# Experts' weights copied from a held set by ScalarE in place of a DMA load per block, from the tenth block on

## The chip, the cores and the metric

The kernel runs on one core of a Trainium2 chip. The metric is device time of one execution in microseconds: 2009.96 us before, the median of three runs (2009.22 to 2015.2). TensorE (PE), VectorE (DVE), ScalarE (ACT), GpSimd (POOL) and SyncE (SP) run their own instruction streams and meet through semaphores. SP and POOL issue the DMA transfers spoken of here.

## The reference

A two-layer graph network over 6250 nodes and 200,000 edges, and behind it a mixture of six experts, with two chosen per node. Cut to what matters:

```python
x = x + gnn(layernorm(x), edges)               # two layers, segment sums over edges
f = layernorm(x)
logits = softmax(relu(f @ router_w1 + b1) @ router_w2 + b2)
top_w, top_i = top_k(logits, 2)
gate = softmax(top_w)
h1 = relu(f @ expert_w1[e] + expert_b1[e])     # 256 -> 256, per expert
h2 = relu(h1 @ expert_w2[e] + expert_b2[e])
out_e = h2 @ expert_w3[e] + expert_b3[e]
x = x + gate[0] * out_e(top_i[0]) + gate[1] * out_e(top_i[1])
```

Everything is float32 at the interface. The change touches the experts' part, the last three products.

## The kernel before

The graph layers come first. Their message sums are products of count matrices with the messages, which the tile `parts` holds in SBUF ([128, 49, 512] in float16). During the sums of the second layer the router works beside them, pair of node tiles by pair, and scatters every node's row twice, into `first_rows` for its first choice and `second_rows` for its second, sorted by expert.

The experts then work in blocks of 256 rows of one expert: 60 blocks, 30 for the first choices (blocks 0 to 29, results scattered to `first_out`) and 30 for the second (blocks 30 to 59, whose base rows are gathered from `first_out` and whose results go to the output). `block_table` in SBUF says for each block its expert and its first row. It is known only at run time, so a table read into a register precedes each use of it.

All of one block's weights and biases are 1796 float32 columns of a packed table in DRAM (`expert_pack`): 514 for the first layer, 514 for the second, 768 for the third with its bias. The tile `w`, a view of a part of the tile `counts_again` that is free by then, has three slots, so block b uses slot b % 3. `rows` has six slots.

On each engine the blocks run skewed. In step b:

- TensorE (`products`, L2166): first layer of block b+2 (from `y_t`, L2126), transposes of block b+3 (`turn`, L2120), second layer of block b+1 (from `h_t`, L2126), third layer of block b (`outs`, L2155).
- ScalarE (`low_halves`, L2211): the lower half of the first layer of block b+2 with bias and relu (`low`, L2202), the copy of `y_t` for block b+3 (`y_copy`, L2198), the lower half of the second layer of block b+1 (L2202).
- VectorE (`high_halves`, L2362): the upper halves (L2320), the token indices (L2342, L2344), bias and base rows (L2325), the normalised rows of block b+4 in the first half (L2349), the gated result (`add_outs`, L2333), which sets `result_ready`.
- GpSimd (`moves`, L2419): two indirect scatters a block, and in the second half two gathers (L2409, L2416).
- SyncE (`loads`, L2080): four transfers in this order, each behind a table read: first weights of block b+5 (`first_weights`, once the first layer of b+2 has been read out of PSUM), second weights of block b+4 (`second_weights`, likewise), third weights of block b+3 and the rows of block b+6 (`load_rows`), both behind `result_ready` of block b.

Semaphore counts order the engines; no planner reorders anything, the order on each engine is the one written. During the first twelve steps `beside(b)` puts the last of the routing between the blocks' instructions: on ScalarE the router's last root, copy, relu and two exponentials in steps 2, 3, 4, 6 and 7. The loops run six blocks a trip; the first twelve blocks and the ends are written out.

Of the kernel before, what the change touches and what calls it, by code (L numbers as in the profile page):

```python
# [17 lines left out]
P = 128  # L18
# [448 lines left out]
def gnn_moe_kernel(nc, x, src, dst, gnn_w, gnn_b, res_w, res_b, router_w1, router_b1, router_w2, router_b2,  # L467
# [35 lines left out]
    with ctx:  # L503
# [765 lines left out]
        def gather_sum(l):  # L1269
# [5 lines left out]
            rows_t_ready = own_sem(f"rows_t_ready{l}")  # L1275
            hs_gathered = own_sem(f"hs_gathered{l}")
            agg_gathered = own_sem(f"agg_gathered{l}")
            summed = own_sem(f"summed{l}")
# [15 lines left out]
            with nc.Block() as block:  # L1294
# [23 lines left out]
                @block.tensor  # L1318
                def _(pe):
                    with pe.Fori(0, cols) as c:  # L1320
                        pe.wait_ge(column_made, ADDED * c + INDEXED)
                        nc.tensor.transpose(bank[0][:, 0:P], gs_dst[:, 0:1].to_broadcast([P, P]), ident[:, :]).then_inc(rows_t_ready, 1)
                        pe.wait_ge(column_made, ADDED * c + SAME)
                        pe.wait_ge(hs_gathered, 16 * c + 16)
                        nc.tensor.matmul(bank[1][:, 0:dim], gs_same[:, :], gs_hs[:, :], start=True, stop=True).then_inc(summed, 1)
# [8 lines left out]
                @block.vector  # L1334
                def _(dve):
                    dve.wait_ge(edges_back, 64)
                    dve.wait_ge(lower_set, 4)
                    with dve.Fori(0, cols) as c:
                        dve.wait_ge(scattered, 16 * c + 16)
                        nc.vector.tensor_copy(index[:, 0:1], src_sb[:, bass.ds(c, 1)]).then_inc(column_made, 1)  # L1340
                        nc.vector.tensor_copy(index[:, 1:2], dst_sb[:, bass.ds(c, 1)]).then_inc(column_made, 1)
                        nc.vector.tensor_copy(gs_dst[:, :], dst_sb[:, bass.ds(c, 1)]).then_inc(column_made, 1)
                        dve.wait_ge(rows_t_ready, c + 1)
                        nc.vector.tensor_scalar(gs_same[:, :], bank[0][:, 0:P], gs_dst[:, 0:1], None, ALU.is_equal).then_inc(column_made, 1)
                        dve.wait_ge(column_made, ADDED * c + SAME)

                        nc.vector.tensor_tensor(gs_before[:, :], gs_same[:, :], lower[:, :], ALU.mult).then_inc(column_made, 1)
                        dve.wait_ge(column_made, ADDED * c + SAME + 1)
                        nc.vector.tensor_reduce(gs_count[:, :], gs_before[:, :], AX, ALU.add).then_inc(column_made, 1)
                        dve.wait_ge(column_made, ADDED * c + SAME + 2)  # L1350
                        nc.vector.scalar_tensor_tensor(gs_count[:, :], gs_count[:, :], float(FAR), gs_dst[:, :], ALU.mult, ALU.add).then_inc(column_made, 1)
                        dve.wait_ge(column_made, ADDED * c + SAME + 3)
                        nc.vector.tensor_copy(index[:, 2:3], gs_count[:, :]).then_inc(column_made, 1)
                        dve.wait_ge(summed, c + 1)
                        dve.wait_ge(agg_gathered, 16 * c + 16)
                        nc.vector.tensor_tensor(gs_agg[:, :], gs_agg[:, :], bank[1][:, 0:dim], ALU.add).then_inc(column_made, 1)
# [602 lines left out]
        def expert_blocks(router, counts):  # L1959
# [13 lines left out]
            acc, result = (both_w[:, l, :, :] for l in range(2))  # L1973
            rows = sb("rows", [P, SB, 2, 2 * dim + 6], F32)
# [24 lines left out]
            rows_loaded = [sem(f"rows_loaded{b}") for b in range(SB)]  # L1999
            normal_ready = sem("normal_ready")  # L2000
# [16 lines left out]
            assert NB % SB == 0 and SB % WB == 0 and SB % 6 == 0  # L2017
# [24 lines left out]
            class Work:  # L2042
# [36 lines left out]

                def loads(self, sp):  # L2080
                    def after(first):
                        def body(b, k):
                            if not (isinstance(b, int) and b + 2 + WB >= BLOCKS):
                                self.first_weights(sp, b + 2, k + 2)
                            if not (isinstance(b, int) and b + 1 + WB >= BLOCKS):
                                self.second_weights(sp, b + 1, k + 1)
                            if isinstance(b, int) and b + WB >= BLOCKS:
                                return
                            e = self.expert_of(sp, b + WB)
                            sp.wait_ge(result_ready, b + 1)  # L2090
                            self.load_weights(sp, e, k, 2)
# [3 lines left out]
                            if first is not None:  # L2095
                                self.load_rows(sp, b + SB, k, first)
# [8 lines left out]
                    for b in range(BLOCKS - SB, BLOCKS):  # L2105
                        after(None)(b, b)
# [104 lines left out]
                def low_halves(self, act, beside):  # L2211
# [5 lines left out]

                    def steps(r, last=False):
                        for k in range(SB):
# [3 lines left out]
                            if not (last and k + 3 >= SB):  # L2223
                                self.y_copy(act, b + 3, (k + 3) % SB)
                            if not (last and k + 1 >= SB):
                                second(b + 1, (k + 1) % SB)
                            if isinstance(b, int) and b < 2 * SB:
                                beside(b)
# [373 lines left out]
```

## Time and profile before

| what | value |
|---|---|
| median of three runs | 2009.96 us (2009.22 to 2015.2) |
| the profiled execution | 2009.25 us |
| its span | 2006.8 us |
| TensorE busy | 1843.3 us, 92% of the span |
| VectorE busy | 1121.0 us, 56% |
| ScalarE busy | 769.0 us, 38% |
| GpSimd busy | 391.2 us, 19% |
| DMA | 412.57 MB, mean 206 GB/s |
| the experts' stage | from about 1610 us to the end, 60 blocks |

The busy shares are averages over stages with different limits. The sums of the graph layers fill the first 1600 us, mostly with TensorE; the change lies in the last 400. Times in the rows are microseconds from the span's start. In a row, `out<-in` names tiles with buffer numbers left out, so `h_t` is the first or the second layer's output and `counts_again` in the experts' stage is the weights' tile. "Issue" marks idle time for which the profile shows no releaser, and "remote" a releaser on another core or an unknown queue.

### The profile page before, as it was taken

To read this page: it belongs to the slowest core of one execution; us is meant where nothing else is said; L and a number is where in the kernel's file an instruction comes from. 1 tells how busy PE (TensorE), PEld (TensorE's weight loads), DVE (VectorE), ACT (ScalarE), POOL (GpSimd) and SP (SyncE) were. 2 spreads that over 40 slices of the span, in tenths; PEclk is the share of its full clock that TensorE was granted. 3 is DMA by queue.
4 is the path that set the end of the run, shared out by engine and by line. 5 is a ranking of instruction groups with operands and counts; after the bars stand their busy time and mean duration, and the time that the engine had idled before them with its cause. 6 is when DMAs were issued, how large, how long until landed. Compare 5 with 4: busy or idle time off the path is not lost. (4 is left out here: it accounts for less than half of the span.)

```text
span 2006.8 us, 35596 instructions
## 1 busy us (share of the span) xinstructions
PE 1843.3 (92%) x11170; PEld 1127.9 (56%) x11170; DVE 1121.0 (56%) x2788; ACT 769.0 (38%) x1686; POOL 391.2 (19%) x403
## 2 busy tenths in 40 slices
PE   4448799999999999999969999999999999989886
PEld 4337655555555555555524444454444478877775
DVE  7247766666666666666513444444444568644443
ACT  2226655665556565556501222222222232222221
POOL 1680000000000000000000112111112123346655
PEclk8679799999999999999979999999999999999998
DMA  6255498899889953323284445554444578877884
GB/s 223 58 85 114 130 322 301 296 349 262 288 283 291 305 179 127 152 88 154 109 324 160 176 170 188 192 203 178 170 175 176 190 230 250 257 220 230 249 246 125
DMA packets 139199, 412.57 MB, mean 206 GB/s; under 512 B 16552, under 2 KB 76928, under 8 KB 132856
## 3 DMA queue, kind: packets, MB, share of 16 engines
q1 hardware_dynamic: 100216, 283.65, 41.3%
q0 software_dynamic: 37904, 124.85, 21.2%
q10 hardware_dynamic: 1008, 3.21, 0.4%
q8 instruction: 33, 0.54, 0.1%
q14 instruction: 38, 0.31, 0.1%
HBM read 201.60 MB, written 219.99 MB: 210 GB/s over the span
## 5 line engine op out<-in xcount | busy, mean ns | idle before, releaser
L1380 PE MATMUL bank<-parts,counts 128*128 128x512 f16 x2401 | 644.4, 379 | 0.0
L1380 PE MATMUL bank<-parts,counts_again 128*128 128x512 f16 x2401 | 540.4, 381 | 17.4 <-DMA counts_again<-counts_table 17.4
L1544 ACT ACTIVATE counts<-bank 128x392 f16<-128x392 f32 x800 | 394.8, 497 | 312.9 <-PE bank L1460 306.2
L1380 PEld LDWEIGHTS bank<-parts,counts_again 128*128 128x128 f16 x2401 | 234.0, 99 | 286.9 <-issue 16.2
L595 DVE TENSOR_TENSOR rows_lo<-pair_keys,iota_lo 128x2048 bf16<-128x2048 bf16 x200 | 244.9, 1224 | 238.5 <-PE bank L1460 238.2
L1460 PEld LDWEIGHTS bank<-rows_hi,rows_lo 128*128 128x128 bf16 x3200 | 229.5, 99 | 202.5 <-issue 27.6
L1460 PE MATMUL bank<-rows_hi,rows_lo 128*128 128x98 bf16 x3200 | 280.0, 211 | 9.5 <-DVE rows_hi L595 8.6
L1380 PEld LDWEIGHTS bank<-parts,counts 128*128 128x128 f16 x2401 | 192.7, 96 | 103.9 <-issue 1.7
L454 POOL DMA_INDIRECT first_rows<-route_rows,route_spot_i x49 | 47.7, 973 | 839.9 <-DVE tokens L445 831.9
L595 DVE TENSOR_TENSOR rows_hi<-pair_keys,iota_hi 128x1568 bf16<-128x1568 bf16 x200 | 193.5, 967 | 0.0
L2202 ACT ACTIVATE h_t<-bank,counts_again 128x256 f32<-128x256 f32 x120 | 56.6, 473 | 210.2 <-PE bank L2126 147.2
L2126 PE MATMUL bank<-h_t,counts_again 128*128 128x256 f32 x480 | 119.1, 393 | 10.6 <-issue 6.6
L912 PE MATMUL bank<-both_w,feat 128*128 128x256 f32 x196 | 64.4, 461 | 60.5 <-issue 37.3
L1396 ACT ACTIVATE middle<-bank 128x256 f32<-128x256 f32 x98 | 37.2, 380 | 213.7 <-PE bank L1380 213.7
L2126 PE MATMUL bank<-y_t,counts_again 128*128 128x256 f32 x480 | 113.8, 380 | 4.7 <-issue 4.7
L2155 PE MATMUL bank<-counts_again,h_t 128*128 128x256 f32 x480 | 114.2, 381 | 0.0
L2320 DVE TENSOR_SCALAR h_t<-bank,counts_again 128x256 f32<-128x256 f32 x120 | 57.6, 480 | 93.7 <-PE bank L2126 48.3
L2126 PEld LDWEIGHTS bank<-h_t,counts_again 128*128 128x128 f32 x480 | 89.5, 196 | 22.5 <-issue 12.0
L2126 PEld LDWEIGHTS bank<-y_t,counts_again 128*128 128x128 f32 x480 | 90.8, 190 | 18.5 <-issue 6.3
L2155 PEld LDWEIGHTS bank<-counts_again,h_t 128*128 128x128 f32 x480 | 91.8, 192 | 12.8
L375 DVE TENSOR_TENSOR route_prob<-bank,router_b_sb 128x12 f32<-128x12 f32 (+1 forms) x25 | 4.2, 170 | 162.6 <-PE bank L365 162.6
L183 PE MATMUL bank<-both_w,x_t 128*128 128x512 f32 x196 | 92.3, 593 | 0.5 <-ACT x_t L173 0.5
(259 smaller groups left out, 1846.6 us busy)
## 6 DMA issues: line engine op xcount, KB each, us to landing
counts_table<-counts SPq DMA_DIRECT2D x25, 3136.0 KB, 10.7
counts_again<-counts_table SPq DMA_DIRECT2D x24, 3136.0 KB, 11.3
first_rows<-zero_rows POOLq DMA_DIRECT2D x3, 10530.0 KB, 58.2
second_rows<-zero_rows POOLq DMA_DIRECT2D x3, 10449.0 KB, 66.7
counts_again<-expert_pack SPq DMA_DIRECT2D x120, 257.0 KB
counts_again<-expert_pack SPq DMA_DIRECT2D x60, 384.0 KB
res_tile<-res_table SPq DMA_DIRECT2D x98, 128.0 KB, 6.2
first_rows<-zero_rows POOLq DMA_DIRECT2D x1, 10270.0 KB, 58.6
```

The source lines that it names most:

```text
L183: mm = nc.tensor.matmul(self.product_bank[:, :], self.x1_t[:, o, k * P:(k + 1) * P], self.both_w[:, self.l + 1, k, :], start=k == 0, stop= ...
L454: pool.indirect_dma_start(table, bass.IndirectOffsetOnAxis(ap=self.spot_i[:, b, c, o:o + 1], axis=0), rows[:, b, o, lo:hi], None, bounds_c ...
L595: return nc.vector.tensor_tensor(rows, k, v, ALU.is_equal)
L912: mm = nc.tensor.matmul(res_bank(t)[:, 0:dim], feat[:, t, k * P:(k + 1) * P], both_w[:, 0, k, dim:2 * dim], start=k == 0, stop=k == K2 - 1)
L1380: mm = nc.tensor.matmul(acc[:, 0:2 * dim], lhs, rhs, start=s == 0, stop=s == tiles)
L1396: nc.scalar.activation(middle[:, o, :], bank[half_bank + o][:, dim:2 * dim], ACT.Copy, scale=1.0 / LOW).then_inc(middle_out, 1)
L1460: mm = nc.tensor.matmul(bank[4 + q % 4][:, u * width:(u + 1) * width], rows_lo[:, r % 2, at, :, u % 2], rows_hi[:, r % 2, at, :, u % 2], s ...
L1544: nc.scalar.activation(counts[:, b, :, :].rearrange("p s (o n) -> p o s n", o=2)[:, :, :, q * QUAD:(q + 1) * QUAD], bank[4 + q % 4][:, 0:Q ...
L2126: mm = nc.tensor.matmul(to[m][:, 0:ROWS], weights_of(k, n)[:, kf, m * P:(m + 1) * P], source[:, k % 2, kf, :], start=kf == 0, stop=kf == K ...
L2155: mm = nc.tensor.matmul(outs_bank[k % 2][:, cols_of], h2_t[:, k % 2, kf, h * P:(h + 1) * P], weights_of(k, 2)[:, kf, :], start=kf == 0, st ...
L2202: nc.scalar.activation(to[:, k % 2, 0, :], frm[0][:, 0:ROWS], ACT.Relu, bias=bias_of(k, n, 0)).then_inc(low_out, 1)
L2320: nc.vector.tensor_scalar(to[:, k % 2, 1, :], frm[1][:, 0:ROWS], bias_of(k, n, 1), 0.0, ALU.add, ALU.max).then_inc(high_out, 1)
```

## The change

A tile view `held` is laid over `parts`, which the sums no longer need: the packed weights of all six experts, 6 x 1796 float32 columns. SyncE loads one expert's weights behind each of the blocks 0 to 5. The weights of blocks 0 to 8 (`LOADED` = 9) are loaded by DMA as before. From block 9 on ScalarE copies a block's three parts from `held` into its slot of `w`, each copy behind a table read of its own, and signals the semaphores that the DMA signalled. SyncE is left with the rows loads. In the branch that is not taken here (a fallback for graphs with many equal edges) two semaphores become one, which frees the number for `held_loaded`.

```diff
+            held = parts[:, :, :].rearrange("p t d -> p (t d)").bitcast(F32)[:, 0:experts * W_COLS].rearrange("p (e n) -> p e n", e=experts)
+            LOADED = 3 * WB
...
+                def hold(self, sp, e):
+                    sp.dma_start(held[:, e, :], expert_pack[e]).then_inc(held_loaded, 16)
...
                         def body(b, k):
-                            if not (isinstance(b, int) and b + 2 + WB >= BLOCKS):
+                            if isinstance(b, int) and b + 2 + WB < LOADED:
                                 self.first_weights(sp, b + 2, k + 2)
-                            if not (isinstance(b, int) and b + 1 + WB >= BLOCKS):
+                            if isinstance(b, int) and b + 1 + WB < LOADED:
                                 self.second_weights(sp, b + 1, k + 1)
-                            if isinstance(b, int) and b + WB >= BLOCKS:
-                                return
-                            e = self.expert_of(sp, b + WB)
-                            sp.wait_ge(result_ready, b + 1)
-                            self.load_weights(sp, e, k, 2)
+                            if isinstance(b, int) and b + WB < LOADED:
+                                e = self.expert_of(sp, b + WB)
+                                sp.wait_ge(result_ready, b + 1)
+                                self.load_weights(sp, e, k, 2)
+                            else:
+                                sp.wait_ge(result_ready, b + 1)
...
-                            if first is not None:
-                                self.load_rows(sp, b + SB, k, first)
+                            self.load_rows(sp, b + SB, k, first)
+                            if isinstance(b, int) and b < experts:
+                                self.hold(sp, b)
...
+                    def weights(b, k, n):
+                        e = act.value_load(block_table[0:1, 0, bass.ds(b, 1)], min_val=0, max_val=experts - 1)
+                        if isinstance(b, int) and b == LOADED:
+                            act.wait_ge(held_loaded, 16 * experts)
+                        if n == 0:
+                            act.wait_ge(h1_high_out, b - (WB - 1))
+                        if n == 1:
+                            act.wait_ge(h2_high_out, b - (WB - 1))
+                        if n == 2:
+                            act.wait_ge(result_ready, b - (WB - 1))
+                        part = slice(W_AT[n], W_AT[n + 1])
+                        nc.scalar.activation(w[:, k % WB, part], held[:, bass.ds(e, 1), part].rearrange("p a n -> p (a n)"),
+                                             ACT.Copy).then_inc(w_loaded[n][k % WB], 16)
+
+                    def held_weights(b, k, n, last):
+                        if not (isinstance(b, int) and b < LOADED) and not (last and k >= SB):
+                            weights(b, k, n)
...
                             if not (last and k + 3 >= SB):
                                 self.y_copy(act, b + 3, (k + 3) % SB)
+                            held_weights(b + 4, k + 4, 0, last)
                             if not (last and k + 1 >= SB):
                                 second(b + 1, (k + 1) % SB)
+                            held_weights(b + 3, k + 3, 1, last)
+                            held_weights(b + 2, k + 2, 2, last)
```

Three places show how the order moves. An "ISA" row is register work or a wait of the instruction stream itself, a "TENSOR_LOAD" is a table read.

The first is ScalarE's loop of six blocks a trip, one step of it. Before:

```order
L2202 ACTIVATE h_t<-bank,counts_again 128x256 [waits h1_ready]
L2197 REGISTER_ALU
L2198 ACTIVATE y_t<-bank 128x512 [waits y_turned]
L2202 ACTIVATE h_t<-bank,counts_again 128x256 [waits h2_ready]
L2201 ISA
```

The same step in the changed kernel, without its last five rows, which are a third copy of 128x768 with its table read and a wait for `result_ready`:

```order
L2207 ACTIVATE h_t<-bank,counts_again 128x256 [waits h1_ready]
L2202 REGISTER_ALU
L2203 ACTIVATE y_t<-bank 128x512 [waits y_turned]
L2224 ISA
L2224 TENSOR_LOAD block_table
L2224 ISA x2
L2234 ISA [waits h1_high_out]
L2234 ACTIVATE counts_again<-parts 128x514
L2207 ACTIVATE h_t<-bank,counts_again 128x256 [waits h2_ready]
L2224 TENSOR_LOAD block_table
L2224 ISA x2
L2234 ISA [waits h2_high_out]
```

One copy now stands between the copy of `y_t` and the second layer's half, two behind that half.

The second is ScalarE in the step of block 5 of the changed kernel, which is written out and holds the first use of the held weights:

```order
L2207 ACTIVATE h_t<-bank,counts_again 128x256 [waits h1_ready]
L2203 ACTIVATE y_t<-bank 128x512 [waits y_turned]
L2224 TENSOR_LOAD block_table
L2224 ISA x2
L2234 ISA [waits h1_high_out,held_loaded]
L2234 ACTIVATE counts_again<-parts 128x514
L2207 ACTIVATE h_t<-bank,counts_again 128x256 [waits h2_ready]
```

The wait for `held_loaded`, all six loads, stands ahead of the second layer's half of block 6.

The third is SyncE in the same step of the changed kernel (`parts<-expert_pack` is the load of one expert's held weights; this is the sixth):

```order
L2049 TENSOR_LOAD block_table
L2049 ISA x2
L2053 ISA [waits result_ready]
L2053 DMA counts_again<-expert_pack 128x768
L2056 TENSOR_LOAD block_table
L2056 ISA x2
L2058 ISA
L2058 DMA rows<-first_rows 128x2x260
L2083 DMA parts<-expert_pack 128x1796
```

The sixth load is issued behind `result_ready` of block 5, block 8's third weights and a rows load. From the next step on SyncE's queue holds only a wait, a table read and the rows load for each block.

## Rows read from the trace of the kernel before

**Rows 1.** Busy time of each engine by stretch, granted clock, DMA share:

```profile
core 0: us, PE busy (x) PEld busy (x) DVE busy (x) ACT busy (x) POOL busy (x), PEclk, DMA share, GB/s
1620.00:1660.00 40.00, 38.34 (x194) 32.90 (x194) 28.67 (x106) 13.14 (x27) 15.92 (x16) 1.00 0.73 223
1690.00:1798.00 108.00, 108.00 (x539) 95.14 (x539) 66.07 (x188) 29.32 (x57) 40.84 (x40) 1.00 0.84 252
1800.00:1820.00 20.00, 14.74 (x64) 12.39 (x64) 7.80 (x21) 2.94 (x7) 14.12 (x14) 0.83 0.52 152
1812.00:1979.00 167.00, 147.74 (x700) 124.79 (x700) 72.05 (x200) 36.95 (x75) 103.13 (x101) 0.98 0.81 244
```

**Rows 2.** Timeline of TensorE (start, length, line, tiles, idle time before):

```profile
1618.52 1.89 PE L2126 MATMUL bank<-y_t,counts_again 128*128 128x256 f32 x8
...
1655.73 1.89 PE L2126 MATMUL bank<-y_t,counts_again 128*128 128x256 f32 x8
...
1657.89 1.89 PE L2126 MATMUL bank<-h_t,counts_again 128*128 128x256 f32 x8
...
1691.77 1.89 PE L2126 MATMUL bank<-y_t,counts_again 128*128 128x256 f32 x8
...
1798.54 1.89 PE L2126 MATMUL bank<-y_t,counts_again 128*128 128x256 f32 x8
...
1806.12 3.75 PE L2126 MATMUL bank<-h_t,counts_again 128*128 128x256 f32 x8 [5.26 <-issue]
...
1811.83 1.89 PE L2126 MATMUL bank<-y_t,counts_again 128*128 128x256 f32 x8
...
1979.07 1.89 PE L2126 MATMUL bank<-y_t,counts_again 128*128 128x256 f32 x8
```

**Rows 3.** Waits, 1800 to 1985 us (waiter, releaser: total us, times, longest):

```profile
DVE h_t L2320 <- remote: 31.3, 7, 6.0
ACT h_t L2202 <- remote: 29.5, 8, 6.1
...
PE bank L2120 <- DMA rows<-second_rows: 11.3, 11, 3.2
```

**Rows 4.** Chain that ended last, 1800 to 2007 us: shares, three pieces of SyncE's queue:

```profile
by line: issue 23.0%; PE bank L2126 13.3%; another core or an unknown queue 10.8%; SPq L2051 8.6%; SPq L2047 8.4%; DMA rows<-second_rows 5.7%; SPq L2054 4.2%; PE bank L2155 3.5%; SPq L2056 3.3%; POOL out_dram L2416 2.8%; DVE h_t L2320 2.3%;
...
1880.11 0.70 SPq L2047
...
1900.31 0.31 SPq L2051
...
1901.38 0.33 SPq L2051
```

**Rows 5.** Table reads by source line (duration in ns, min/median/max):

```profile
L2047 SPq TENSOR_LOAD <-block_table x180: 3/269/1006, 1606.7 to 1977.1; - x180
...
L2545 ACTq TENSOR_LOAD <-flag x1: 477/477/477, 225.5 to 225.5; - x1
```

**Rows 6.** DMA issues, 1250 to 2007 us (count, size each, us to landing):

```profile
counts_again<-counts_table SPq DMA_DIRECT2D x15, 3136.0 KB, 11.2
counts_again<-expert_pack SPq DMA_DIRECT2D x120, 257.0 KB
counts_again<-expert_pack SPq DMA_DIRECT2D x60, 384.0 KB
...
rows<-first_rows SPq DMA_DIRECT2D x30, 260.0 KB
```

**Rows 7.** Groups of ScalarE, SBUF to SBUF (busy us, mean ns, idle before):

```profile
L156 ACT ACTIVATE x<-layer_sum 128x256 f32<-128x256 f32 x49 | 20.2, 412 | 2.9 <-DVE layer_sum L133 2.0
...
L870 ACT ACTIVATE parts<-both_w 128x2048 f32<-128x2048 f32 x1 | 1.9, 1897 | 0.0
```

**Rows 8.** Timeline of ScalarE, two activations in a row:

```profile
1814.73 0.47 ACT L2202 ACTIVATE h_t<-bank,counts_again 128x256 f32<-128x256 f32 x1 [6.06 <-PE bank L2126]
1815.10 0.59 ACT L2198 ACTIVATE y_t<-bank 128x512 f32<-128x512 f32 x1
```

**Rows 9.** Timeline of VectorE, the result of block 5:

```profile
1656.03 0.88 DVE L2333 SCALAR_TENSOR_TENSOR both_w<-bank,rows,both_w 128x256 f32<-128x256 f32 x2 [0.90 <-PE bank L2155]
```

More of the change, by code:

```diff
@@ L1274, in gather_sum @@
             INDEXED, SAME, ADDED = 3, 4, 9
-            rows_t_ready = own_sem(f"rows_t_ready{l}")
+            turned_or_summed = own_sem(f"turned_or_summed{l}")
             hs_gathered = own_sem(f"hs_gathered{l}")
             agg_gathered = own_sem(f"agg_gathered{l}")
-            summed = own_sem(f"summed{l}")
             scattered = own_sem(f"scattered{l}")
@@ L1321, in _ @@
                         pe.wait_ge(column_made, ADDED * c + INDEXED)
-                        nc.tensor.transpose(bank[0][:, 0:P], gs_dst[:, 0:1].to_broadcast([P, P]), ident[:, :]).then_inc(rows_t_ready, 1)
+                        nc.tensor.transpose(bank[0][:, 0:P], gs_dst[:, 0:1].to_broadcast([P, P]), ident[:, :]).then_inc(turned_or_summed, 1)
                         pe.wait_ge(column_made, ADDED * c + SAME)
                         pe.wait_ge(hs_gathered, 16 * c + 16)
-                        nc.tensor.matmul(bank[1][:, 0:dim], gs_same[:, :], gs_hs[:, :], start=True, stop=True).then_inc(summed, 1)
+                        nc.tensor.matmul(bank[1][:, 0:dim], gs_same[:, :], gs_hs[:, :], start=True, stop=True).then_inc(turned_or_summed, 1)
                 @block.sync
@@ L1342, in _ @@
                         nc.vector.tensor_copy(gs_dst[:, :], dst_sb[:, bass.ds(c, 1)]).then_inc(column_made, 1)
-                        dve.wait_ge(rows_t_ready, c + 1)
+                        dve.wait_ge(turned_or_summed, 2 * c + 1)
                         nc.vector.tensor_scalar(gs_same[:, :], bank[0][:, 0:P], gs_dst[:, 0:1], None, ALU.is_equal).then_inc(column_made, 1)
@@ L1353, in _ @@
                         nc.vector.tensor_copy(index[:, 2:3], gs_count[:, :]).then_inc(column_made, 1)
-                        dve.wait_ge(summed, c + 1)
+                        dve.wait_ge(turned_or_summed, 2 * c + 2)
                         dve.wait_ge(agg_gathered, 16 * c + 16)
@@ L1999, in expert_blocks @@
             rows_loaded = [sem(f"rows_loaded{b}") for b in range(SB)]
+            held_loaded = sem("held_loaded")
             normal_ready = sem("normal_ready")
@@ L2016, in expert_blocks @@
             first_back = [sem(f"first_back{b}") for b in range(3)]
-            assert NB % SB == 0 and SB % WB == 0 and SB % 6 == 0
+            assert experts <= SB and LOADED - 4 >= experts - 1 and NB % SB == 0 and SB % WB == 0 and SB % 6 == 0
             assert 2 * SB <= EARLY_BLOCKS + 1 <= 3 * SB
@@ L2104, in loads @@
                     rounds(sp, NB - SB, BLOCKS - SB, after(False))
-                    for b in range(BLOCKS - SB, BLOCKS):
-                        after(None)(b, b)
                 def turn(self, pe, b, k, r, second=False):
```

## The prediction

> **What bounds the kernel now.** I read the busy time by stretch first. From 1690 to 1798 us, where the first choices' blocks run alone, TensorE (PE) is busy 108.00 of 108.00 us; from 1812 to 1979 us, the second choices' blocks, it is busy 147.74 of 167.00 us, at almost the same DMA share, 0.81 against 0.84 [rows 1]. So the experts' stage has two halves with different limits. The TensorE timeline gives the pace: each block has one group of eight passes from y_t, and from one such group to the next is one block. Twenty groups stand from 1691.77 to 1798.54 us: 106.77 / 19 = 5.62 us a block. Twenty-six stand from 1811.83 (block 34) to 1979.07 us (block 59): 167.24 / 25 = 6.69 us [rows 2]. The products of a block are the same in both, so the second half loses 25 x (6.69 - 5.62) = 26.7 us. The first blocks, beside the last routing, lose a little: 1618.52 (block 2) to 1655.73 us (block 8) is 37.21 us, 6.20 a block [rows 2].
>
> The list of waits says what the 26.7 us are. TensorE waits 11.3 us, in 11 waits, for rows that come late from second_rows. VectorE and ScalarE stand 31.3 and 29.5 us before their halves of h_t with a releaser that the profile can't name ("remote"), up to 6.1 us at once, and TensorE then waits for them [rows 3]. The same list for 1690 to 1798 us names neither. The rows are late because SyncE's queue is: the chain that ended last runs through its lines L2051 and L2047 for 8.6% and 8.4% of the time after 1800 us, more than through the last product (L2155, 3.5%). In this stretch one instruction of L2047 can take 0.70 us [rows 4]; its table read has a median of 0.269 us [rows 5]. SyncE issues four transfers a block in strict order, three of weights, each behind a wait, and the rows last; even undisturbed, two such issues stand 1.07 us apart (1900.31 and 1901.38) [rows 4].
>
> What makes signals and instructions late I can only bound: it happens where most is written into SBUF by DMA. A block's weights are 257 + 257 + 384 = 898 KB, its rows 260 [rows 6]; the second half adds a gather of 256 rows of 1 KB.
>
> **What the change removes.** From block 9 on, no weights by DMA: 51 blocks x 898 KB, and on SyncE three of four issues a block, with their table reads and waits. What DMA writes into SBUF falls in the second half from about 1414 to 516 KB a block, under the 1158 KB of the first half, which runs at 5.62 us without a late row. The gain lies between 11.3 us (late rows alone [rows 3]) and all 26.7. I take **-26.7**: the first half, with more traffic than what stays, is the nearest row and loses nothing.
>
> **What it adds on ScalarE.** Three copies a block, of 514, 514 and 768 columns, SBUF to SBUF. Two rows give the price: 256 columns take 412 ns, 2048 take 1897 ns, so 0.829 ns a column and 626 + 626 + 836 ns = 2.09 us [rows 7]. Ahead of each stand a table read, register work and a wait; SyncE's 1.07 us from issue to issue less 0.33 us for the issue itself gives 0.74 [rows 4], 2.22 for three. The activations that were there take 0.47 + 0.59 + 0.47 = 1.53 us [rows 8]. If nothing overlaps, that is 5.84 us, just over a block's 5.62. But ScalarE runs ahead: the copy of y_t at 1815.10 us starts before the activation of 1814.73 us has ended [rows 8]. If each read hides behind some 0.5 us of the activation before it, the sum is 4.3. The copies' own waits (slots read by blocks done a step before) are met when they are reached. Behind the first copy stands the second layer's half of h_t, moved back by at most 0.74 + 0.63 us; TensorE wants it only behind the next block's first layer. Cost in the steady blocks: **0**, hidden under TensorE; without that cover the excess over 5.62 counts on every block.
>
> **The new wait.** The six loads of all experts' weights are put behind the first six blocks on SyncE, each after that block's result and its rows load. ScalarE waits for all six in the step of block 5, after the copy of y_t for block 8 and ahead of the second layer's half for block 6. Queued behind it: that half, then everything else on ScalarE. TensorE's second layer of block 7, at 1657.89 us here [rows 2], needs it. The sixth load can't be issued before block 5's result, which ends at 1656.03 + 0.88 = 1656.91 us [rows 9]; ahead of it SyncE issues block 8's third weights and a rows load, so 1658.9. Lower bound: an empty queue. 3136 KB land in 11.2 us [rows 6], so 898 KB take 3.2: 1662.1; then copy (0.63), half (0.47) and handovers, 1.3: 1663.4, a stop of 5.5 us. Likely: 384 + 260 KB go first at the 223 GB/s (218 KB per us) of this stretch [rows 1]: (384 + 260 + 898) / 218 = 7.1 us; 1658.9 + 7.1 + 1.3 = 1667.3, a stop of 9.4. Upper: the fifth load still under way too, and signals late by up to 6 us: 18. I take **+10**. TensorE restarts slowly: after a wait of 5.26 us its group at 1806.12 us took 3.75 us where 1.89 is usual, and from there to 1811.83 us two groups took 5.71 us [rows 2] where a steady block's two take 3.46, half speed (1.2 of 2.4 GHz) for that first group, and a granted clock of 0.83 over the 20 us around it [rows 1]: **+2.3**.
>
> **Smaller terms.** The six loads crowd the first steps: 6 x 898 KB more, while weights for blocks 3 to 8 are still loaded. If those six steps fall from 6.20 to the second half's 6.69 us: 6 x 0.49 = **+3** (from 0, as weights come two steps ahead, to 8, if transfers set the pace for some of them). The router's last exponential, in the step of block 6, stands behind one more copy on the path to its choices: **+1** (0 to 1.4). The renamed semaphores of the other branch and the end of SyncE's loop, which loses its last six steps: 0; neither is reached or waited for.
>
> **Sum.** 2009.25 (the profiled execution; its span is 2006.8, 2.45 lies around it; 0.7 under the median of 2009.96) - 26.7 + 10 + 2.3 + 3 + 1 = 1998.9, so **1999 us**.
>
> **Rivals.** *The stands stay.* If the late signals come from the gathers and scatters, which remain, or GpSimd's four indirect transfers a block pace the half (busy 103.13 of 167 us [rows 1]), only the late rows go: 2009.25 - 11.3 + 16.3 = 2014. For it: the stands are frequent only where the gathers are. Against: SyncE, which issues no gather, is slow with them, and GpSimd is free for 38% of that stretch. 0.2.
>
> *ScalarE becomes the pace*, and the end is slower. Place: its loop of six blocks; it decides once the sum passes 5.62 us. Unhidden the sum is 5.84; ScalarE's one table read here, the flag's, took 0.477 us, not 0.269 [rows 5], and with three of these it is 6.46. At the middle, 6.15, the first half's 25 periods from block 7 on cost 0.53 more each (+13.3), the second half gains only 25 x (6.69 - 6.15) = 13.5, and the total is 2009.25 + 13.3 - 13.5 + 16.3 = 2025 (2010 and 2041 at the ends). Against: the overlap above [rows 8], and that ScalarE has idle time in every block now. 0.14. The Trainium skill, "DMA: Bandwidth & Descriptors", section "Latency and other measured facts", gives a floor of about 600 ns for a tensor_load; by that floor the unhidden sum would be 6.8 us and the total, an estimate, 2060. The median of 0.269 us here [rows 5] disagrees with it.
>
> *The wait hardly counts*: the sixth load lands after the lower bound and the first steps don't slow: 2009.25 - 26.7 + 5.5 = 1988. 0.08.
>
> **How the numbers follow.** The forecast has 0.58, with 1990 to 2006 as its own span. A measurement of this kernel tells 0.3%, 6 us, from no change: faster is under 2004, slower over 2016. Faster: 0.5 of the forecast's 0.58 and the short wait's 0.08, 0.58. Same: the rest of the forecast and some of the stands that stay, 0.2. Slower: ScalarE's pace, and stands that stay with a first stage that costs more than I bound, 0.22. The range 1988 to 2016 leaves out most of ScalarE's 0.14 and the ends of the others.
>
> **What would show it.** Right: 5.6 us a block in the second half, no waits for second_rows and no "remote" there, and one stop of TensorE some 10 us long near block 7, released through ScalarE by the loads of expert_pack. Wrong: block periods over 5.7 us in the first half with ScalarE busy throughout (second rival); "remote" still in the second half (first rival); no stop at block 7.

## The result, and the profile after

The changed kernel takes 2017.8 us (median of 8 runs) beside 2010.22 us for the kernel before on the same chip: 1.0037 times as long, 95% interval 1.0021 to 1.0052. One of its eight runs, at 2819.42 us with a granted clock of 0.65, was a slow one that the ratio and its interval leave out; the median of the other seven is 2016.0 us. The forecast of 1999 us was wrong, and so was its side.

The profiled execution of the changed kernel took 2019.65 us, with a span of 2017.4, so 10.6 us more span than before. Three sources show where they are. The first is busy time by stretch, to be read beside [rows 1].

```profile
core 0: us, PE busy (x) PEld busy (x) DVE busy (x) ACT busy (x) POOL busy (x), PEclk, DMA share, GB/s
1620.00:1660.00 40.00, 36.39 (x186) 31.25 (x184) 28.62 (x105) 10.92 (x22) 15.95 (x16) 1.00 0.87 304
1660.00:1690.00 30.00, 20.18 (x88) 17.07 (x89) 13.75 (x54) 12.68 (x24) 4.22 (x5) 0.83 0.31 113
1690.00:1798.00 108.00, 107.86 (x537) 94.72 (x537) 72.54 (x215) 65.22 (x116) 41.99 (x42) 1.00 0.30 90
1824.00:1986.00 162.00, 148.74 (x702) 127.72 (x701) 71.85 (x200) 84.00 (x149) 100.32 (x97) 0.96 0.36 110
```

In the second half (last line) DMA now moves 110 GB/s where it moved 244, and TensorE still has 13 us of idle time in 162. The second source is TensorE's timeline, to be read beside [rows 2].

```profile
1618.76 1.89 PE L2131 MATMUL bank<-y_t,counts_again 128*128 128x256 f32 x8
...
1655.87 1.89 PE L2131 MATMUL bank<-y_t,counts_again 128*128 128x256 f32 x8
...
1668.40 3.75 PE L2131 MATMUL bank<-h_t,counts_again 128*128 128x256 f32 x8 [10.20 <-ACT h_t L2207]
1671.94 2.56 PE L2160 MATMUL bank<-counts_again,h_t 128*128 128x256 f32 x8
1674.34 1.89 PE L2131 MATMUL bank<-y_t,counts_again 128*128 128x256 f32 x8
...
1811.49 1.89 PE L2131 MATMUL bank<-y_t,counts_again 128*128 128x256 f32 x8
1824.15 1.89 PE L2131 MATMUL bank<-y_t,counts_again 128*128 128x256 f32 x8
...
1986.16 1.89 PE L2131 MATMUL bank<-y_t,counts_again 128*128 128x256 f32 x8
```

The groups from `y_t` are those of blocks 2 (1618.76), 8 (1655.87), 9 (1674.34), 33, 34 and 59. From block to block this gives:

| stretch | before, us | after, us | difference |
|---|---|---|---|
| start to block 2 | 1618.52 | 1618.76 | +0.24 |
| block 2 to 8 | 37.21 | 37.11 | -0.10 |
| block 8 to 9 | 5.62 | 18.47 | +12.85 |
| block 9 to 33 | 137.19 | 137.15 | -0.04 |
| block 33 to 34 (change of halves) | 13.29 | 12.66 | -0.63 |
| block 34 to 59 | 167.24 (6.69 a block) | 162.01 (6.48 a block) | -5.23 |
| block 59 to the end | 27.73 | 31.24 | +3.51 |

So one stop of 12.85 us is new, and the second half gives back only 5.2 us. The end of the run, from block 59's group on, is 3.5 us longer. The third source is the list of waits, first for 1655 to 1690 us, then for 1820 to 1990 us (to be read beside [rows 3]).

```profile
ACT counts_again L2234 <- DMA parts<-expert_pack: 14.4, 1, 14.4
...
PE bank L2131 <- ACT h_t L2207: 10.2, 1, 10.2
```

```profile
DVE h_t L2346 <- remote: 32.7, 9, 4.7
...
ACT h_t L2207 <- remote: 26.5, 7, 5.7
...
DVE both_w L2359 <- remote: 23.8, 9, 4.3
```

ScalarE's first copy waits 14.4 us for the held loads, and TensorE 10.2 us behind it. In the second half no wait for `second_rows` is left, but the stands (idle stretches of an engine, put down to "remote") are as long as before. One of them, from the timeline of 1844 to 1861 us:

```profile
1848.61 0.60 PE L2125 MATMUL bank<-ident,rows 128*128 128x128 f32 x4
...
1857.33 0.60 ACT L2203 ACTIVATE y_t<-bank 128x512 f32<-128x512 f32 x1 [6.63 <-remote]
```

ScalarE's copy of `y_t` waits for TensorE's transposes. They had ended at 1849.21 us, ScalarE was idle from 1850.70, and the copy began at 1857.33, 8.1 us after the work that it waited for was done. Whether the signal came late or ScalarE answered it late, the rows don't tell; "late signals" below stands for both.

### The profile page after: what moved, and what is told of

Same layout as the page of the kernel before. It is cut to its first block and busy times, and to the rows that moved or that the text cites. A ratio compares the mean times of both kernels' runs of the same rounds, so it can differ in the third digit from the quotient of the medians.

```text
span 2017.4 us, 35373 instructions
## 1 busy us (share of the span) xinstructions
PE 1848.2 (92%) x11170; PEld 1134.1 (56%) x11170; DVE 1119.4 (55%) x2788; ACT 865.2 (43%) x1840; POOL 390.7 (19%) x403
## 5 line engine op out<-in xcount | busy, mean ns | idle before, releaser
L1379 PEld LDWEIGHTS bank<-parts,counts_again 128*128 128x128 f16 x2401 | 233.7, 99 | 284.4 <-issue 14.4
L2131 PE MATMUL bank<-h_t,counts_again 128*128 128x256 f32 x480 | 118.5, 391 | 17.8 <-ACT h_t L2207 10.2
L2131 PE MATMUL bank<-y_t,counts_again 128*128 128x256 f32 x480 | 118.6, 392 | 11.2 <-ACT y_t L2203 11.2
L2234 ACT ACTIVATE counts_again<-parts 128x514 f32 x153 | 105.3, 700 | 23.8 <-DMA parts<-expert_pack 14.4
L2131 PEld LDWEIGHTS bank<-y_t,counts_again 128*128 128x128 f32 x480 | 93.5, 196 | 26.7 <-ACT y_t L2203 12.4
```

Of the source, the lines that this page charges most:

```text
L1379: mm = nc.tensor.matmul(acc[:, 0:2 * dim], lhs, rhs, start=s == 0, stop=s == tiles)
L2131: mm = nc.tensor.matmul(to[m][:, 0:ROWS], weights_of(k, n)[:, kf, m * P:(m + 1) * P], source[:, k % 2, kf, :], start=kf == 0, stop=kf == K ...
L2234: nc.scalar.activation(w[:, k % WB, part], held[:, bass.ds(e, 1), part].rearrange("p a n -> p (a n)"), ACT.Copy).then_inc(w_loaded[n][k % ...
```

## The experiments

Two questions were put to the chip: whether the stop hangs on where ScalarE waits, and what makes the stands. Block periods below are read from TensorE's timeline as in the table above; "the second half" is block 34 to block 59, and the tail is what follows block 59's group. late_wait, late12 and the three pause runs were run several times; every other kernel below was run once, and in those runs the block periods say more than the time.

**late_wait: the wait five blocks later.** Edit of the changed kernel:

```diff
-            LOADED = 3 * WB
+            LOADED = 5 * WB - 1
```

> The change with the switch from DMA loads to held weights five blocks later: blocks 9 to 13 are loaded by DMA as well, and ScalarE's wait for the six held loads stands before block 14's weights. If the 12.85 us between block 8 and block 9 are that wait and nothing else, they fall to 5.62 to 7 us, no half-clock restart is left there, the second half keeps its 6.48 us a block, and the time is 2017.8 - 12 = about 2006 us (2004 to 2009), 0.997 to 0.9995 of the kernel before. Rival: the held loads crowd the DMA engines whatever waits for them, the block loads of blocks 9 to 13 come late instead, and 6 us or more of the stop remain (2012 us or more).

Measured: 2005.64 us (10 runs) beside 2010.82 us, ratio 0.9977 (0.9964 to 0.9990). Its timeline at blocks 8 and 9:

```profile
1660.51 1.89 PE L2131 MATMUL bank<-y_t,counts_again 128*128 128x256 f32 x8
1666.13 1.89 PE L2131 MATMUL bank<-y_t,counts_again 128*128 128x256 f32 x8
```

The period is 5.62 us again, although DMA is about as busy as in the changed kernel (301 GB/s from 1623 to 1661 us). The stop was the place of the wait, not the traffic. The second half stays at 6.52 us a block. Its tail is 26.5 us; over all runs here tails lie between 23.6 us (plain_scatter) and 37.6 us (four_paced), so the 3.5 us of the changed kernel's tail don't come with the held weights as such; ScalarE stands 4.9 us "remote" in it, and the rest is open.

**late12: the wait three blocks later** (`LOADED = 4 * WB`).

> The change with blocks 9 to 11 loaded by DMA as well, so that ScalarE's wait for the held loads stands three blocks later instead of five. If the sixth held load lands within three blocks more, the stop is gone as in the run with five, and the time is the same 2005.6 us within 2 us. If the extra block loads push it later than that, 2 to 6 us of the stop are left and the time is 2008 to 2012 us.

Measured: 2007.99 us (10 runs) beside 2011.23 us, ratio 0.9990 (0.9980 to 1.0000). Block 8 to 9 is 5.62 us here too, and no later block has the stop, so the sixth load lands within three blocks more. The 2.4 us to late_wait are not clear of noise: the two intervals overlap.

**no_gather and before_no_gather: no gathers in the second half**, from the changed kernel and from the kernel before. The edit is the same in both, and drops the gathers at the loop's ends too:

```diff
-                            if c:
-                                dve.wait_ge(first_back[k % 3], ...)
...
                     def second(b, k):
-                        self.gather(pool, b + 2, k + 2)
                         self.scatter(pool, b, k, out)
```

> The change without the second half's gathers and the wait for them (the earlier sums are not added to the second half's rows, so that addition is left out). Theory: the stands that the trace calls remote come with the gathers, the only work of GpSimd that the first half doesn't have; without them the second half runs at 5.62 us a block, 25 blocks take 140.5 us where they took 162, and the time is about 2017.8 - 21 = 1997 us (1993 to 2000). Rival A: scatters, or anything both halves have, make the stands once the rows are small; then 6.2 to 6.5 us a block and 2010 us or more. Rival B: half of each, 6.0 us a block, 2005 us.

> The kernel before, weights by DMA, without the second half's gathers and the wait for them (that addition is left out). If the gathers alone make the stands, its second half falls from 6.69 to 5.62 us a block and the time to about 2010 - 27 = 1983 us, so that weight traffic costs nothing without gathers. If the weight loads cost something of their own, 5.8 us a block or more is left (1988 us or more). If neither, it stays near 6.7 us (2009 us).

Measured: 1989.80 and 1978.27 us. Busy time by stretch in the second half, first of the changed kernel without gathers, then of the kernel before without them:

```profile
1820.00:1950.00 130.00, 130.00 (x651) 114.60 (x650) 68.29 (x186) 78.10 (x139) 46.86 (x47) 1.00 0.30 91
```

```profile
1810.00:1940.00 130.00, 130.00 (x649) 114.55 (x648) 67.89 (x186) 35.80 (x70) 47.15 (x47) 1.00 0.84 256
```

TensorE is busy all the time in both, at 5.62 us a block (140.48 / 25). The second line decides the prediction's main term: the weights' transfers run at 256 GB/s, and without the gathers they cost nothing. Both times are lower than expected because the change of halves (block 33 to 34), which waits for the first gathers, falls to 5.62 us as well. The pair also prices the change without any stands: it loses 11.5 us (1989.80 against 1978.27), as the stop is there (19.20 us from block 8 to 9) and the second half has nothing to give back.

**plain_gather: the same bytes by plain transfers.** Edit of the changed kernel:

```diff
-                        pool.indirect_dma_start(rows[:, k % SB, h, X2], None, first_out, ...).then_inc(...)
+                        pool.dma_start(rows[:, k % SB, h, X2], first_out[h * P:(h + 1) * P, :]).then_inc(...)
```

> The change with each gather replaced by a plain transfer of the same 128 rows of 1 KB from fixed rows of the same table, issued by the same engine at the same place (the earlier sums that are added are then other rows' sums). If the bytes or the issuing at that place make the stands, the second half stays at 6.3 to 6.5 us a block (about 2016 us). If it is the indirect form, it falls to 5.62 to 5.8 us (about 1998 us).

Measured: 1989.76 us and 5.62 us a block. Bytes and place are the same, so it is the indirect form, or the longer time that it takes on GpSimd (1.04 us each in the changed kernel, where a plain one takes 0.59).

**small_gather: still indirect, 128 bytes a row.** The gathers read `first_out` viewed as rows of 32 numbers.

> The change with gathers of 128 bytes a row instead of 1 KB, still 128 indirect rows each (the sums that are added are then not the earlier ones). If the stands come from the number of indirect transfers, they stay: 6.2 to 6.6 us a block, 2010 us or more. If they come from the gathered bytes, the pace falls to 5.7 us or less and the time to 1998 us or less.

Measured: 2020.32 us, 6.58 us a block. The waits of 1830 to 1950 us:

```profile
DVE h_t L2346 <- remote: 26.8, 9, 4.1
...
ACT h_t L2207 <- remote: 19.4, 6, 4.4
ACT y_t L2203 <- remote: 19.2, 4, 5.2
```

With an eighth of the bytes the stands are still there.

**plain_scatter: indirect gathers, plain scatters.** This asks whether it is the reading. The condition `table is out` confines the edit to the second half:

```diff
-                        pool.indirect_dma_start(table, ..., result[:, k % 2, cols_of], None, ...).then_inc(...)
+                        (pool.dma_start(table[(2 * k + h) * P:(2 * k + h + 1) * P, :], result[:, k % 2, cols_of]) if table is out else
+                         pool.indirect_dma_start(table, ..., result[:, k % 2, cols_of], None, ...)).then_inc(...)
```

> The change with its second half's scatters made plain transfers of the same size to fixed rows of the output (the output's order is then not computed), its gathers left indirect. Theory 1: four indirect transfers a block leave GpSimd no pause, and the signals of all engines fall behind while it issues them; with two a block, whichever two, the second half runs at 5.62 us a block and the time is 1990 us (1988 to 1993), as without gathers. Theory 2: it is the gathers' own doing (indirect reads); then 6.3 to 6.5 us a block stay, 2012 us or more.

Measured: 1994.81 us, 5.62 us a block; the time lies above the 1988 to 1993 us expected, as the gathers keep the change of halves at 12.58 us. Two indirect transfers a block make no stands, gathers or scatters; the gathers by themselves are not the cause.

**gathers_in_first_half: stands where there were none.** The kernel before with two more indirect transfers in each of blocks 18 to 29 (and two ahead of them), each pair behind the landing of the pair before:

```diff
+                        for h in range(2):
+                            pool.indirect_dma_start(spare[...], None, first_rows, ..., to_token[:, k, h:h + 1], ...)
```

> The kernel before, with two indirect gathers a block more in blocks 18 to 29 of the first half (rows of the first table into unused space; nothing reads them). Theory 1: four indirect transfers a block make the same stands in the first half, 6.2 to 6.8 us a block where there were 5.62, so 12 blocks take 7 to 14 us longer and the time is about 2021 us. If the stands need something that only the second half has (small row loads, the second table, reads of rows just written), these blocks stay at 5.62 to 5.75 us and the time at 2010 to 2012 us.

Measured: 2016.69 us. TensorE's timeline at blocks 25, 26, 32 and 33, and the waits of 1690 to 1811 us:

```profile
1753.09 1.89 PE L2126 MATMUL bank<-y_t,counts_again 128*128 128x256 f32 x8
1763.53 3.75 PE L2126 MATMUL bank<-y_t,counts_again 128*128 128x256 f32 x8 [4.66 <-issue]
...
1803.20 3.44 PE L2126 MATMUL bank<-y_t,counts_again 128*128 128x256 f32 x8 [2.83 <-issue]
1810.58 1.67 PE L2126 MATMUL bank<-y_t,counts_again 128*128 128x256 f32 x7
```

```profile
ACT h_t L2202 <- remote: 14.3, 3, 6.8
DVE h_t L2320 <- remote: 11.2, 5, 3.3
```

Two stands of the known kind, with TensorE groups of 3.75 and 3.44 us behind them where 1.89 is usual, put 12.5 us between block 25 and block 33 (57.49 us where the kernel before has 44.96). ScalarE's first long stand begins at 1751.17 us, 21 us after the first extra transfer (1729.72). Nothing that only the second half has is needed. The time is 4 us below the 2021 us expected.

The kernel before has a stand of the same kind in its own first half, where there are no gathers. From 1639.78 to 1648.84 us GpSimd issues eight indirect scatters, about 1.3 us apart (two of a block's results, four of the router's, two of a block's results), and in the timeline of 1638 to 1653 us stand

```profile
1639.78 0.97 POOL L2416 DMA_INDIRECT first_out<-both_w,to_token  x1 [5.59 <-DVE both_w L2333]
...
1643.76 0.60 PE L2120 MATMUL bank<-ident,rows 128*128 128x128 f32 x4
...
1648.39 0.60 ACT L2198 ACTIVATE y_t<-bank 128x512 f32<-128x512 f32 x1 [4.82 <-remote]
1648.84 0.97 POOL L2416 DMA_INDIRECT first_out<-both_w,to_token  x1 [0.30 <-issue]
...
1651.31 0.48 DVE L2320 TENSOR_SCALAR h_t<-bank,counts_again 128x256 f32<-128x256 f32 x1 [4.26 <-remote]
```

Here the copy is 4 us behind transposes that ended at 1644.36 us, VectorE stands 4.3 us as well, and ScalarE's stand begins (1643.57 us) 3.8 us after the first of the eight, not 21.

**three_indirect, filled_gpsimd, three_filled: number or busyness.** One gather of two plain (from the changed kernel); both gathers plain and two fills of 925 numbers added (from the kernel before); one gather plain and two fills of 360 numbers (from the changed kernel). The last one's edits:

```diff
                     for h in range(2):
-                        pool.indirect_dma_start(rows[:, k % SB, h, X2], None, first_out, ...).then_inc(...)
+                        (pool.dma_start(rows[:, k % SB, h, X2], first_out[0:P, :]) if h == 0 else
+                         pool.indirect_dma_start(rows[:, k % SB, h, X2], None, first_out, ...)).then_inc(...)
...
                     def second(b, k):
+                        pool.wait_ge(passed, ...)
+                        pool.sem_inc(passed, 1)
+                        nc.gpsimd.memset(weighed[...], 0.0).then_inc(passed, 1)
+                        nc.gpsimd.memset(past[...], 0.0).then_inc(passed, 1)
                         self.gather(pool, b + 2, k + 2)
```

> The change with one of a block's two gathers made a plain transfer from fixed rows (half of the sums that are added are then other rows' sums): three indirect transfers a block, GpSimd some 4.9 us busy of 5.62. If the stands need GpSimd nearly without pause, they go: 5.62 to 5.7 us a block, 1990 to 1995 us. If they grow with each indirect transfer, about half of the excess stays, 6.0 us a block and 2004 us.

> The kernel before with plain transfers in place of the second half's gathers (other rows' sums are added then), and two fills of 925 numbers a block more on GpSimd, about 1.9 us, which make it as busy as four indirect transfers do (5.2 to 5.5 us of 5.62). If GpSimd's mere busyness makes the stands, they stay: 6.3 us a block or more, 2000 us or more. If it is the issuing of indirect transfers, the second half stays near 5.62 us a block (up to 5.75) and the time is 1979 to 1984 us, by the kernel before without gathers at 1978.3.

> The run with three indirect transfers a block, with two fills of 360 numbers (0.8 us) more on GpSimd, which make it busy 5.5 us of 5.62, as four indirect transfers do. If a fourth indirect transfer makes the stands, there are none here: 5.62 us a block or whatever GpSimd allows (up to 5.8), 1990 to 1996 us. If it is GpSimd without a pause while indirect transfers run, stands come back: 6.1 us a block or more, 2003 us or more.

Measured: 1991.89, 1980.96 and 1997.80 us, all three at 5.62 us a block in the second half. Busy time by stretch, first of filled_gpsimd, then of three_filled, and three_filled's groups on GpSimd in the same stretch (busy, mean ns, idle before):

```profile
1830.00:1930.00 100.00, 100.00 (x500) 88.10 (x500) 52.59 (x142) 27.62 (x54) 85.43 (x106) 1.00 0.93 301
```

```profile
1830.00:1950.00 120.00, 120.00 (x599) 105.73 (x598) 63.09 (x170) 72.91 (x131) 94.22 (x130) 1.00 0.45 137
```

```profile
L2443 POOL DMA_INDIRECT out_dram<-both_w,to_token x44 | 45.5, 1034 | 21.3 <-issue 16.7 <-POOLq L2458 2.7 <-DVE both_w L2359 1.9
L2436 POOL DMA_INDIRECT rows<-first_out,to_token x21 | 22.4, 1068 | 6.4 <-issue 5.5 <-DVE both_w L2359 0.9
```

GpSimd is busier than in the changed kernel (85% and 79% against 100.32 of 162 us, 62%), in the first beside 301 GB/s of DMA, and there are no stands. In three_filled it issues four transfers a block too, one of them plain, and waits for other engines under 3 us in 120 (1.9 and 0.9 in its rows). So neither a busy GpSimd nor its number of transfers is the cause; the fourth indirect one in 5.62 us is.

**four_paced: four indirect transfers, slowly.** The kernel before with the two fills of 925 numbers ahead of the gathers:

> The kernel before with its four indirect transfers a block in the second half and two fills of 925 numbers (1.8 us) ahead of each block's gathers: GpSimd then needs about 7.1 us a block and sets the pace. If the stands come from too many indirect transfers in a stretch of time, they end here: 7.1 to 7.2 us a block, steady, with waits for GpSimd's work in place of those called remote, 25 blocks in 178 to 181 us. If four in a row make a stand whatever pause follows, remote waits remain and the pace is uneven, over 7.4 us a block on the mean.

Measured: 2018.05 us, 6.64 us a block on the mean. The waits of 1830 to 1950 us:

```profile
ACT h_t L2202 <- PE bank L2126: 66.8, 22, 4.1
DVE both_w L2325 <- DMA rows<-first_out,to_token: 50.5, 17, 3.6
```

No "remote" wait is in that list, nor in the one of the whole second half: VectorE waits openly for gathered rows. The pace was a miss. GpSimd goes at an even 6.87 us a block (its first gathers of 1824.18 to 1906.61 us, 12 blocks), not 7.1: the two fills take 1.70 us, and the gather behind them comes after 0.16 us, where I had counted 0.30. TensorE's mean is lower still, as its first three periods are 5.62 us. That the stands end when the four come slower holds.

**pause_short, pause_long, pause_two: a version that uses it.** The late wait, with a fill ahead of each block's gathers: 120 numbers (0.22 us), 360 (0.42), and two of 360 (0.83). The first one's edit beside that of late_wait:

```diff
                     def second(b, k):
+                        pool.wait_ge(passed, 4 * (b - NB) + NB + 2)
+                        pool.sem_inc(passed, 1)
+                        nc.gpsimd.memset(weighed[...][:, 0:120], 0.0).then_inc(passed, 1)
                         self.gather(pool, b + 2, k + 2)
```

> The late wait (DMA loads up to block 13), and in the second half a fill of 120 numbers on GpSimd ahead of each block's gathers, about 0.2 us in which it issues nothing: its four indirect transfers take 5.32 us, so the pace it allows is about 5.6 to 5.7 us a block. If the signals fall behind because GpSimd issues indirect transfers with hardly a pause, some of the stands go: 5.7 to 6.2 us a block, 25 blocks 7 to 20 us less than with the late wait alone, 1986 to 1999 us. If a short pause lets nothing drain, 6.5 us or more stay: 2006 to 2010 us.

> The same with a fill of 360 numbers, about 0.45 us, which makes GpSimd the slowest engine at 5.8 to 5.95 us a block. If the pause lets signals through, the second half runs steadily at that: (6.48 - 5.9) x 30 = 17 us less than with the late wait alone, about 1988 us (1985 to 1996). If stands come as before, the pace is 6.5 to 6.9 us a block and the time 2006 to 2018 us.

> The late wait with two fills of 360 numbers on GpSimd (0.83 us) ahead of each block's gathers in the second half: GpSimd needs 4 x 1.33 + 0.83 = 6.15 us a block. If the stands end as soon as indirect transfers come no faster than that, 0.65 in a us where they stayed at 0.70 with the fill of 0.42 us and were gone at 0.60, the pace is 6.1 to 6.2 us with no waits called remote, and the time 1996 to 2001 us, at or below the runs with shorter fills. If 0.65 in a us is still too many, remote waits stay and the pace is 6.3 us or more, 2002 us or more.

| run | us | beside | ratio (95%) | second half, us a block |
|---|---|---|---|---|
| late_wait | 2005.64 | 2010.82 | 0.9977 (0.9964 to 0.9990) | 6.52 |
| pause_short | 2001.83 | 2008.18 | 0.9974 (0.9964 to 0.9984) | 6.32 |
| pause_long | 2002.03 | 2008.18 | 0.9968 (0.9955 to 0.9982) | 6.34 |
| pause_two | 2004.66 | 2016.21 | 0.9942 (0.9925 to 0.9960) | 6.38 |

All beat the kernel before, by 0.2 to 0.6%. Only pause_two's interval lies apart from late_wait's, and just so; the other two overlap with it. The pace of the profiled runs doesn't rank the three. For late_wait, and then for pause_two, the waits of 1820 to 1975 us say:

```profile
DVE h_t L2346 <- remote: 47.7, 12, 6.3
...
ACT y_t L2203 <- remote: 13.3, 4, 6.0
```

```profile
DVE h_t L2346 <- remote: 44.1, 19, 3.9
ACT y_t L2203 <- remote: 25.5, 12, 3.5
```

So the stands became shorter and more frequent and did not end. pause_short and pause_long fit neither of their expectations, as their 6.32 and 6.34 us a block lie between the two; pause_two came out by its second.

How close may indirect transfers follow each other? With fills and gathers back to back, GpSimd's own pace is some 6.0 us for four in pause_two (gathers at 1869.30 and 1875.26 us), where stands remain, and 6.87 us in four_paced, where none do; no run lies between. Counts over a whole stretch don't separate the two kinds, because a stand holds GpSimd back as well: from block 34 to 59 the kernel before, with stands, issues 101 indirect transfers in 167.2 us, and four_paced, without, 98 in 165.9. That there is a limit of some 0.6 a us, and that the stands are how the excess is paid, is a reading that would fit; no run shows it.

## Why the prediction was wrong

**The failed step** is the first term of the sum, -26.7 us for the second half, with its reason that signals are late where DMA writes most into SBUF. It measured -5.2 (in late_wait and late12 the second half takes 163.1 and 162.7 us, and with loads by DMA 165.2 in gathers_in_first_half, so the gain is 2 to 5 us). I took the first half, with more bytes than what stays and no stands, as the nearest row; but what made the difference between the halves was the number of indirect transfers, four a block against two. [rows 1] spoke against DMA traffic as the cause already: it was 252 GB/s in the first half, without stands, and 244 in the second, with them. Without the gathers the kernel before runs its second half at 5.62 us with all its weight transfers at 256 GB/s. The bound from below (11.3 us for late rows) failed too: those waits did vanish, but the half became only 5.2 us shorter, with the stands as long as before. So taking a wait away need not give its time back; where the other 6 us went was not followed up.

**The rival "the stands stay"** named the cause, GpSimd's gathers and scatters, and had 0.2. Its evidence, that stands are frequent only where the gathers are, pointed the right way, though the stand at 1643.57 us shows that scatters alone make one too. What I held against it, that GpSimd is free for 38% of the stretch, says nothing: three_filled shows a busier GpSimd with no stands. Its 2014 us took 11.3 us off the second half where 5.2 came off.

**The wait, +10, and the restart, +2.3**, were right: together 12.3 us, where block 8 to block 9 grew by 12.85. TensorE's wait of 10.2 us was released through ScalarE by the loads. Behind it a group took 3.75 us at half the usual speed, in a stretch with a granted clock of 0.83, and two groups 5.94 us (1668.40 to 1674.34) instead of 3.46. late_wait takes just these away: the changed kernel is 7.6 us above the kernel before run beside it, late_wait 5.2 below. Their place was named, and so it could have been asked whether the wait has to stand there.

**The crowded first steps, +3**, were 0: block 2 to 8 took 37.11 us with 304 GB/s instead of 223. The router's **+1** can't be told from the stop.

**ScalarE's copies, 0**, were right. From block 14 (1704.72 us) to block 33 the pace is 5.62 us, as before, with ScalarE busy 65.22 of 108 us. By line, its table reads (min/median/max ns) and its copies:

```profile
L2224 ACTq TENSOR_LOAD <-block_table x153: 271/278/461, 1651.8 to 1989.5; - x153
```

```profile
L2234 ACT ACTIVATE counts_again<-parts x153: 618/633/849, 1667.2 to 1990.1; 128x514 f32 x102, 128x768 f32 x51
```

The copies of 514 columns cost 0.63 us, as priced from [rows 7]. A table read on ScalarE takes 0.278 us, like SyncE's, and not the 0.477 us by which the second rival reached its upper end. Nor is the sum of 5.84 us without any overlap reached, as the pace of 5.62 us shows. The Trainium skill gives a floor of about 600 ns for a tensor_load ("DMA: Bandwidth & Descriptors", section "Latency and other measured facts"); the 153 reads here disagree with it.

**The sum and the chances.** With the second half and the stop as measured the sum is 2009.25 - 5.2 + 12.85 = 2016.9 us; the tail, which the prediction did not have in its sum, makes up most of what is left to the profiled 2019.65. The prediction gave 0.22 to a time over 2016 us, for ScalarE's pace or for stands that stay beside a dearer first stage. The stands did stay, but the first stage was cheaper than forecast, so that side came about by another way: the second half gained less than the late rows. The third rival's 1988 us leaves out the restart; with it the sum would be 1990.

## What to carry to other kernels

When two stretches differ, list what else differs between them before naming the largest number, here bytes a block, as the cause; leaving one suspect out of the kernel before (before_no_gather) would have settled it without the change. A wait on a bulk load belongs as late as its data allow: five blocks turned 0.4% of loss into 0.2% of gain. Count the indirect transfers that a stage issues and their distance; in these runs four in 5.62 us were too many, three were not, and the loss appeared as late signals on engines that issue none.

## What was not expected of the hardware

- Four indirect transfers of 128 rows in 5.62 us go with stands of up to 6.6 us on ScalarE and 4.7 on VectorE (changed kernel), the longest behind work that was long done; three don't, with GpSimd 79% busy (three_filled), and with 128 bytes a row four still do (small_gather). What in the transfer holds the others back stays open, also whether their signals or their instructions are late.
- Some time passes before a stand: in gathers_in_first_half the first long one came 21 us after the first extra transfer, in the kernel before one came 3.8 us after the first of eight in a row. What sets this was not tried.
- A fill of 0.42 or 0.83 us on GpSimd, of no use to the computation, goes with a shorter second half in the profiled runs (6.34 and 6.38 us a block against 6.52); in the time only the one of 0.83 lies apart from late_wait by its interval.
- Not tried: a mixed order of first and second choices' blocks, which would bring the mean to three indirect transfers a block.
